# A four-layer cross-attention kernel: the probabilities of three attentions are transposed by VectorE and a trip through DRAM instead of TensorE, under a new order of work

## The reference, cut to what matters

```python
# layer 0 (x, context): attentions 0 (self, causal) and 1 (on the context), then a small MLP
x1 = layernorm(x + mha(x, x, causal));   x2 = layernorm(x1 + mha(x1, context))
x3 = layernorm(x2 + relu(x2 @ fc1 + b) @ fc2 + b)      # masked by rows that are all zero
# layer 1: attention 2 (rotary, 4 key heads of 64), then a gated MLP
q, k, v = rmsnorm(x3) @ Wq, rmsnorm(context) @ Wk, rmsnorm(context) @ Wv
p = softmax(rope(q) @ rope(k).T / 8 + mask);  x4 = x3 + (p @ v) @ Wo
x5 = x4 + (silu(n @ Wgate) * (n @ Wup)) @ Wdown        # n = rmsnorm(x4)
# layer 2: attention 3, on layer-normed inputs;   layer 3: attention 4, scores scaled and clipped
x6 = x5 + softmax(Q @ K.T / 4) @ V @ Wo + bo
out = layernorm(x6 + softmax(clip(f(mask) * Q @ K.T / 4)) @ V @ Wo + bo) * gamma + beta
```

## Time and profile before

| | before |
|---|---|
| time, median of 3 runs (range) | 4003.32 us (4002.51 to 4005.87) |
| profiled execution: its own span | 3996.0 us |
| median less span | 7.3 us |
| PE busy | 3939.4 us (99%) |
| DVE busy | 2932.9 us (73%) |
| ACT busy | 2676.8 us (67%) |
| POOL busy | 1233.8 us (31%) |
| 16 DMA engines, share of the main queue | 5.0% |
| TensorE's clock, mean granted share | 0.999 |

### The profile page before, as it was taken

How to read it: one execution, slowest core, us unless ns; L and a number is a source line. 1 busy time by engine, 2 the same in 40 slices (tenths; PEclk the granted TensorE clock), 3 DMA queues, 4 the chain that set the end, 5 groups by cost and what they waited for, 6 DMA issues and landing times.

```text
span 3996.0 us, 116007 instructions
## 1 busy us (share of the span) xinstructions
PE 3939.4 (99%) x44820; PEld 3452.9 (86%) x44820; DVE 2932.9 (73%) x10721; ACT 2676.8 (67%) x8449; POOL 1233.8 (31%) x2247
## 2 busy tenths in 40 slices
PE   7999999999999999999999999999999999999998
PEld 7888888888888888888888888888888888888886
DVE  4677777777777777777777777777777777777764
ACT  3676766776766766767767767667667667676663
POOL 1233333233232332333332332323323333323321
PEclk9999999999999999999999999999999999999999
DMA  3000000000000000000000000000000000000000
GB/s 146 5 15 18 10 18 18 10 18 17 10 18 17 10 18 16 12 18 10 18 18 10 17 18 10 18 18 10 18 17 11 18 10 18 18 10 18 18 3 5
DMA packets 66498, 69.65 MB, mean 17 GB/s; under 512 B 7456, under 2 KB 64800, under 8 KB 65056
## 3 DMA queue, kind: packets, MB, share of 16 engines
q1 hardware_dynamic: 65952, 62.25, 5.0%
HBM read 53.83 MB, written 8.39 MB: 16 GB/s over the span
## 4 chain that ended last, share of the span: by engine, by line
PE 89%; DVE 6%; ACT 2%; issue 1%; POOL 1%; DMA 0%; SPq 0%; DVEq 0%; POOLq 0%; ACTq 0%
PE gen_ps L513 54%; PE gen_ps L505 16%; PE gen_ps L635 6%; PE scores_ps L609 5%; PE gen_ps L647 3%; PE scores_ps L595 3%; PE scores_ps L602 2%; PE scores_ps L588 1%; ACT oT L747 1%; DVE wide L935 1%; DVE zn L980 1%; DVE v L1040 1%; DVE rdenm L977 1%; DVE res L1044 1%; DVE plainT L1043 1%
## 5 line engine op out<-in xcount | busy, mean ns | idle before, releaser
L513 PE MATMUL gen_ps<-actT,w_sb 128*128 128x128 f32 x10752 | 1345.7, 278 | 12.2 <-DMA w_sb<-weights_dram 8.3
L513 PEld LDWEIGHTS gen_ps<-actT,w_sb 128*128 128x128 f32 x10752 | 1261.4, 192 | 67.6 <-issue 47.4
L836 POOL TENSOR_TENSOR rstd<-ve,consts 128x1 f32<-128x1 f32 x448 | 283.4, 633 | 1421.7 <-DVE ve L987 842.1
L747 ACT ACTIVATE probT<-gen_ps 128x512 f32<-128x512 f32 x1024 | 577.2, 634 | 210.5 <-PE gen_ps L505 207.3
L781 ACT ACTIVATE prob<-scores_ps,negmax 128x128 f32<-128x128 f32 x2048 | 568.6, 417 | 199.0 <-DVE negmax L1025 198.9
L505 PE MATMUL gen_ps<-consts,prob 128*128 128x128 f32 x4096 | 598.3, 276 | 11.4 <-ACT prob L781 5.7
L505 PEld LDWEIGHTS gen_ps<-consts,prob 128*128 128x128 f32 x4096 | 467.4, 141 | 122.1 <-ACT prob L781 57.2
L513 PE MATMUL gen_ps<-w_sb,wide 128*128 128x256 f32 x2056 | 465.4, 379 | 0.9 <-DVE wide L1165 0.6
L513 PE MATMUL gen_ps<-w_sb,actT 128*128 128x256 f32 x1792 | 462.5, 381 | 2.7 <-ACT actT L747 2.1
L897 POOL TENSOR_SCALAR prob<-prob,rden 128x128 f32<-128x128 f32 x1024 | 366.7, 380 | 314.7 <-DVE rden L1098 314.7
L747 ACT ACTIVATE actT<-gen_ps 128x256 f32<-128x256 f32 (+1 forms) x512 | 238.8, 466 | 285.0 <-PE gen_ps L505 284.9
(11 more groups left out here) (118 smaller groups left out, 6085.0 us busy)
## 6 DMA issues: line engine op xcount, KB each, us to landing
actT<-xT_dram SPq DMA_DIRECT2D x64, 128.0 KB, 2.2
ctx_rms<-x_dram SPq DMA_DIRECT2D x64, 128.0 KB, 2.2
ctx<-ctx_dram SPq DMA_DIRECT2D x64, 128.0 KB, 2.2
ctxT<-ctxT_dram SPq DMA_DIRECT2D x64, 128.0 KB, 2.3
mask<-mask_dram SPq DMA_DIRECT2D x128, 64.0 KB, 2.1
out_dram<-res SPq DMA_DIRECT2D x64, 128.0 KB, 1.7
w_sb<-weights_dram SPq DMA_DIRECT2D x2, 2048.0 KB, 18.8
w_sb<-weights_dram SPq DMA_DIRECT2D x2, 1024.0 KB, 20.5
```

Source lines behind the costliest of these rows:

```text
L513: last = nc.tensor.matmul(ps, lhsT(c), rhs(c), start=(c == 0), stop=(c == chunks - 1))
L747: release(nc.scalar.activation(dst, take(act, name, b)[:, 0:width], ACT.Copy), name, b)
L836: nc.gpsimd.tensor_tensor(dst, src, const("expo")[:, 0:width], ALU.pow)\
```

## The change

The change has five parts.

1. `BY_VECTOR = (0, 1, 2)`: in these attentions `turn` leaves PE and ACT. DVE transposes each unit in blocks of 32 by 32, reading every fourth column, into `turned`; SP sends `turned` to DRAM (`send`), waits for it to land, and fetches it back with 512-byte pieces into `probT` (`fetch`). Attention 3 keeps the transposes on PE.
2. Six batches in flight (`G` = 6), with fewer slots for the large buffers (`N_WIDE`, `N_K`, `N_V`, ...), two slots of `probT`, and waits for these slots.
3. The two multiplications after the rms norms, the one after the layer norm ahead of attention 3, the scaling of queries of attentions 0 and 1 and the copy of V of attention 2 move from DVE to ACT. Adding the epsilon ahead of `rsqrt` moves to POOL as an instruction of its own.
4. The filler matmuls `BESIDE` go.
5. A new table `LIFE` (with SP's steps in it), and `count_plan` gives each use the bank that the table frees first.

```diff
-PERIOD = 69.731652
+PERIOD = 54.157375
-    ("turn", 0, 0, {"PE": 56.166, "ACT": 82.488}),
+    ("turn", 0, 0, {"DVE": 11.735}),
+    ("send", 0, 0, {"SP": 49.119}),
+    ("fetch", 0, 0, {"SP": 54.289}),
...
+            def turn(a, b, u):
+                n = turned_unit(a, b, u)
+                if a == 2:
+                    dve.wait_ge(sem("normed"), U * b + u + 1)
+                else:
+                    dve.wait_ge(sem("exp_done"), unit(a, b, u) + 1)
+                if n >= N_T:
+                    dve.wait_ge(sent_sem(n), 16 * (n // N_T))
+                nc.vector.transpose(turned[:, n % N_T, :, :, :].rearrange("p t k j -> p k t j"),
+                                    prob[:, u, :, :].rearrange("p k (i t) -> p k t i", t=R)).then_inc(sem("turned"), 1)
...
+                def send(a, b, u):
+                    n = turned_unit(a, b, u)
+                    k = T_OF[a, b]
+                    sp.wait_ge(sem("turned"), n + 1)
+                    if k >= N_FAR:
+                        fetched(sp, *TURNED[k - N_FAR], u)
+                    sp.dma_start(turned_d[n % (U * N_FAR)].rearrange("q (i t) x -> (q i) (t x)", t=R),
+                                 turned[:, n % N_T, :, :, :].rearrange("p t k j -> p (t k j)"))\
+                        .then_inc(sent_sem(n), 16)
+                def take_back(a, b, u):
+                    n = turned_unit(a, b, u)
+                    sp.wait_ge(sent_sem(n), 16 * (n // N_T + 1))
+                    probT_read(sp, a, b)
+                    sp.dma_start(probT[:, TURN_OF[a, b] % N_PT, u, :, :],
+                                 turned_d[n % (U * N_FAR)].rearrange("q t x -> t q x")).then_inc(fetched_sem(a, b, u), 16)
...
+                elif name == "queries":
+                    ps = take(act, f"m{a}", b)[:, 0:D].rearrange("p (c s) -> p c s", c=C)
+                    first_read(act, f"m{a}", b)
+                    q_free(act, a, b)
+                    for e in range(2):
+                        ins = nc.scalar.activation(qT[:, Q_PLACE[a, b] % N_Q, :, e, :], ps, ACT.Copy,
+                                                   scale=const("parityq")[:, e:e + 1])
...
-            def rsqrt(src, dst, wait, signal, b, width=1):
+            def rsqrt(src, dst, eps, wait, signal, b):
                 pool.wait_ge(sem(wait), b + 1)
-                nc.gpsimd.tensor_tensor(dst, src, const("expo")[:, 0:width], ALU.pow)\
-                    .then_inc(sem(signal), 1)
+                nc.gpsimd.tensor_scalar(dst, src, eps, 0.0, ALU.add, ALU.add).then_inc(sem("padded"), 1)
+                padded[0] += 1
+                pool.wait_ge(sem("padded"), padded[0])
+                nc.gpsimd.tensor_tensor(dst, dst, const("expo")[:, 0:1], ALU.pow).then_inc(sem(signal), 1)
...
+    free, full, read, out = [-1e9] * N_GEN, [0] * N_GEN, [0] * N_GEN, {}
...
+            j = min(range(N_GEN), key=lambda j: free[j])
```

More of the change, by code:

```diff
@@ L30 @@
 H = 16
-G = 4
-NG = B // G
+G = 6
+N_WIDE = 2
+N_CTXT = 3
+N_Q = 3
+N_V = 4
+N_K = 4
+N_PT = 2
+BY_VECTOR = (0, 1, 2)
+N_T = 4
+N_FAR = 4
+N_PEN = 4
 U = 4
@@ new lines @@
+    ("ctx_norms", 0, 0, {"DVE": -69.650, "POOL": 113.059}),
+    ("load_ctx", 0, 0, {"SP": -34.396}),
+    ("load_x", 0, 0, {"SP": -3.979}),
+    ("keys", 0, 0, {"ACT": -3.539, "PE": 1.042}),
+    ("queries", 0, 0, {"ACT": 2.043, "DVE": 0.929, "PE": 0.000}),
+    ("first_row", 0, 0, {"DVE": 4.089, "PE": 2.261}),
+    ("soft", 0, 0, {"ACT": 10.808, "DVE": 6.728}),
+    ("scores", 0, 0, {"PE": 7.773}),
+    ("soft", 0, 1, {"ACT": 13.125, "DVE": 7.775}),
+    ("soft", 0, 2, {"ACT": 20.502, "DVE": 11.059}),
@@ new lines @@
+    ("send", 0, 0, {"SP": 49.119}),
+    ("send", 0, 2, {"SP": 50.256}),
+    ("send", 0, 1, {"SP": 50.292}),
+    ("send", 0, 3, {"SP": 50.691}),
+    ("fetch", 0, 0, {"SP": 54.289}),
+    ("keys", 1, 0, {"ACT": 57.227, "PE": 55.229}),
+    ("queries", 1, 0, {"ACT": 57.303, "DVE": 56.884, "PE": 56.350}),
+    ("first_row", 1, 0, {"DVE": 60.344, "PE": 56.439}),
+    ("fetch", 0, 3, {"SP": 58.719}),
+    ("fetch", 0, 2, {"SP": 59.631}),
+    ("fetch", 0, 1, {"SP": 60.479}),
+    ("scores", 1, 0, {"PE": 65.361}),
@@ new lines @@
+    ("norm", 1, 0, {"DVE": 110.924}),
+    ("x2T", 1, 0, {"ACT": 112.604, "PE": 111.011}),
+    ("h", 1, 0, {"ACT": 114.462, "PE": 113.642}),
+    ("send", 1, 0, {"SP": 114.955}),
+    ("z", 1, 0, {"DVE": 115.769, "PE": 117.034, "POOL": 129.844}),
+    ("fetch", 1, 0, {"SP": 116.742}),
+    ("send", 1, 2, {"SP": 117.449}),
+    ("send", 1, 1, {"SP": 117.499}),
+    ("norm_x3", 1, 0, {"ACT": 120.075, "DVE": 118.282}),
+    ("tr", 2, 0, {"ACT": 128.803, "PE": 118.996}),
+    ("send", 1, 3, {"SP": 120.279}),
@@ new lines @@
+    ("nb4", 3, 0, {"DVE": 202.062}),
+    ("fetch", 2, 1, {"SP": 203.129}),
+    ("fetch", 2, 2, {"SP": 203.245}),
+    ("norm_x4", 3, 0, {"ACT": 203.894}),
+    ("tr", 3, 0, {"ACT": 204.281, "PE": 205.204}),
+    ("fetch", 2, 3, {"SP": 205.056}),
+    ("keys", 3, 0, {"ACT": 209.450, "PE": 207.864}),
+    ("queries", 3, 0, {"DVE": 209.450, "PE": 209.078}),
+    ("soft", 3, 0, {"ACT": 212.477, "DVE": 215.168}),
+    ("scores", 3, 0, {"PE": 215.469}),
+    ("soft", 3, 1, {"ACT": 215.713, "DVE": 217.762}),
@@ L178 @@
+    ("zT", 4, 0, {"ACT": 264.302, "PE": 261.779}),
+    ("o", 4, 0, {"DVE": 276.466, "PE": 273.264, "POOL": 291.107}),
+    ("norm", 4, 0, {"DVE": 286.008}),
+    ("store", 0, 0, {"SP": 326.071}),
 ]
@@ L407, in read_out @@
         def read_out(eng, name, i):
-            j, use = plan[name, i]
-            once(eng, bank_read[j], use)
+            j, full, read, before = plan[name, i]
+            once(eng, bank_read[j], read)
         def x_in_sem(b):
@@ L481, in begin @@
             def begin(name, b):
[L483 to L485 removed]
+                j, full, read, before = plan[name, b]
+                if before:
+                    once(pe, bank_read[j], before)
                 return gen_ps[:, j, :]
[L488 to L497 removed]
             def end(ins, name, b):
```

678 lines of the change are left out of this document (361 added, 317 removed).

## The result

The changed kernel takes **4067.5 us** (4053.1 to 4078.5) against 4003.5 us before: a ratio of 1.0156, 95% interval 1.0133 to 1.0180. It is slower. The forecast was 3755 us with a range from 3610 to 3960, so both the range and the sign were missed. The profiled execution has a span of 4071.0 us.

The account below looks back on a forecast made before the run. TensorE, busy 3088 of 3100 us, was taken as the bound. Per batch 60.8 - 5.9 + 1.8 = 56.7 us; 63 x 56.7 + 175 (ends) + 7 (span to median) = 3754, forecast as 3755 us, range 3610 to 3960.

Parts of the forecast that it names:

- Transposes off TensorE: TensorE, steady pace: 48 transposes per batch leave, saving 5.9 us; TensorE alone then needs 54.9 us per batch.
- A wait of 1.8 us ahead of `h`: TensorE waits ahead of `h` for ScalarE's copy of `x2T`: 0.4 to 3.0 us per batch, put at 1.8.
- Ahead of the first row I had named idle time: Sign of being right: TensorE's idle time stands ahead of first-row products and `h`, behind ScalarE's copies.
- the sentence behind it: Outside the stretch walked to `h`, ScalarE and VectorE are ahead of TensorE by a microsecond or more.
- Transposes on VectorE: VectorE: twelve transposes per batch at 0.68 us each, giving 49.6 us of work per batch.
- My rival: VectorE: reading every fourth column makes a transpose cost 1.2 us; 3874 us in all; chance 0.20.
- The rival's consequence: With slow transposes VectorE is the bound at 55.7 us per batch, 58.6 with waits.
- The trip: Send and fetch through DRAM: about 5.5 us, attention 2 the tightest with over 6 us available; costed at nothing.
- The rival named the mechanism: SyncE's in-order queue: trips over 8 us make TensorE wait at `out2`; at 13 us, 4069 us; chance 0.12.
- The 7.5 us for a halved rate: A trip's length if the 512-byte pieces halve the transfer rate.
- Ends: Fill and drain: 175 us out of 150 to 205, from trips 15 more, transposes 18 less, fillers' clock 20.
- The rival that joined a slow transpose to a wait for trips: No net change: slow transposes plus some wait for trips give 60.6 us per batch; chance 0.05.

Follow-up runs that it names:

- e4: Changed kernel with neighbouring columns for VectorE's transposes and no trip through DRAM (products take wrong numbers): 3879.5 us, ratio 0.9694.
- e6: Changed kernel with SyncE's sends of attentions 0 and 1 in the order of the turns, attention 1's ahead of its first fetch: 3953.6 us, ratio 0.9879.
- e9: e7 with attention 3's scores on TensorE moved behind the next batch's queries and keys: 3922.8 us, ratio 0.9800.
- e13: e7 with attention 3's scores on TensorE moved behind the next batch's queries alone: 3823.7 us, ratio 0.9557.
- e5: Changed kernel with ScalarE's copy of attention 2's values ahead of its copies of attentions 4 and 1's products: 3968.4 us, ratio 0.9916.
- e1: Changed kernel with ScalarE writing probabilities so that VectorE's transposes read neighbouring columns, not every fourth: 4017.7 us, ratio 1.0039.
- e10: Kernel before the change with its fillers taken out (BESIDE empty), nothing else: 4019.9 us, ratio 1.0042.
- e3: Changed kernel without sends and fetches; VectorE writes into probT, three slots instead of two (products take wrong numbers): 3921.7 us, ratio 0.9799.
- e7: Changed kernel with the edits of e1, e5 and e6 together: 3833.0 us, ratio 0.9573.
- e8: e7 with 166 filler products added in the first batches alone: 3826.8 us, ratio 0.9559.
- e11: e7 with the second batch's attention 0, up to its trip, 40 us earlier in every engine's list: 3829.0 us, ratio 0.9570.
- e12: e7 with attention 0 of the second batch 25 us earlier and of the third 12 us earlier: 3828.0 us, ratio 0.9570.

## Why the prediction was wrong

My span was 3748 us, the measured one is 4071, 323 us more. Of these 63 x (60.75 - 56.7) = 255 us lie in the pace and 244 - 175 = 69 in the ends.

**Transposes off TensorE: right.** 54.9 us per batch were forecast for TensorE alone and are 54.9 in e4. In the changed kernel itself it is 55.7, because its clock falls behind the long waits (last section); this I had no term for. Waits for trips are the ones in question: e6, which has none, is at 54.9 too.

**A wait of 1.8 us ahead of `h`: not there, but hidden.** Ahead of `h` TensorE idles 0.1 us in the mean. The stretch that I walked, from the end of attention 2's scores (here 2104.44) to `h`, has the waits, but elsewhere:

```profile
2100.64 3.80 PE L648 MATMUL scores_ps<-plainT,wide 32*128 32x128 f32 x64 [0.93 <-POOL plainT L995]
2109.93 1.17 PE L662 MATMUL scores_ps<-plainT,qT 32*128 32x128 f32 x32 [1.01 <-DVE qT L1049]
2117.89 0.71 PE L569 MATMUL gen_ps<-plainT,q 128*128 128x128 f32 x4 [0.84 <-DVE q L1041]
2120.24 1.16 PE L569 MATMUL gen_ps<-actT,w_sb 128*128 128x128 f32 x8
```

Over the 47 batches the stretch takes 15.7 us, 1.7 of them idle, and ScalarE is busy in 14.4. My count had 13.8 to 15.4 for ScalarE and a wait of 1.8, but VectorE, which I had not walked there, holds TensorE first; that the wait's size agrees is chance. (Ahead of the first row I had named idle time, but behind ScalarE.) Where e9 and e13 take VectorE's first wait away, ScalarE's list holds TensorE in its place. The failed step is the sentence behind it, that elsewhere ScalarE and VectorE are ahead of TensorE by a microsecond or more: I had followed ScalarE alone through one stretch, and four of the five waits above end with VectorE, ScalarE or GpSimd. The dearest, 1.45 us, is of the same sort as the one that I walked: a copy that a list holds behind another copy. e5 takes it out with one number.

**Transposes on VectorE: 0.68 taken, 1.11 measured.** My rival had the price and the reason: e1, with neighbours, has 0.70. That is also what the Trainium skill ("SBUF — State Buffer", the note on cachelines under "Door 1") says, that a read which leaves the 16-byte line at each element pays; the trace agrees, with 1114 against 705 ns. The rival's consequence was wrong, though. VectorE did not become the bound (88% busy); being later cost 1.17 us per batch, through single waits.

**The trip: 5.5 us with time to spare, costed at nothing.** For attention 2 this holds (5.9 us, no wait at `out2`). I called it the tightest and did not walk attentions 0 and 1. The rival named the mechanism, a fetch that waits for its own send and holds the sends behind it, but at `out2`, and with no loss against the kernel before until a trip takes 12 us. It stands at attention 1's values products, whose trips take 10.7 us in the mean, and costs 1.9 us per batch (e6). That this rival's 4069 us met the measured time is chance: its pace was 61.7 and its ends were 182. (The 7.5 us for a halved rate should be 5.5 + 2 x 0.84 = 7.2; nothing rested on it, and the rate was not halved, as the last section shows.)

**Ends: 175 us taken, 244 measured.** Four kernels make a ladder: before 167; without fillers 187 (e10); changed but without trips 217 (e3); with trips 244. Fillers cost 20 us on the kernel before, as I allowed; put back into e7 and e13 they gave nothing that can be told. Trips cost 27 where I counted 15. The first store comes at 312.5 us, in e3 at 267.9, 15 us for each of three trips, but the drain is shorter. TensorE's wait for the first values products shows one of them, first in the changed kernel, then in e3:

```profile
43.43 1.94 PE L699 MATMUL gen_ps<-probT,v 128*32 128x128 f32 x32 [17.27 <-DMA probT<-turned_dram]
33.47 1.94 PE L674 MATMUL gen_ps<-probT,v 128*32 128x128 f32 x32 [7.51 <-DVE probT L1118]
```

The step from e10 to e3 holds all the rest of the change at once, the new table and six batches in flight among it: 30 us where I had 18 less for fewer transposes. In the fill it is more: the first store moves from 208.3 us (e10) to 267.9, and the drain gives half of that back. Which part of the first batches' chain holds it stays open: neither fillers (e8) nor earlier work of the next batches (e11, e12) gave it back. A wider move of whole batches in the table was not tried.

**Chances.** Slower had 0.13. The rival that joined a slow transpose to a wait for trips had 0.05, and its pace of 60.6 us is the one that came (60.75). That too is in part chance: with both taken out (e4) 58.16 us stay, so the two explain 2.6 of the 5.9 us above 54.9, and the waits of the order the rest. I had treated the two mainly as exclusive, though nothing in the trace of before said so; and both it and the forecast rested on ends of 175 to 182 us.
